# A two-layer attention kernel: opening of the first layer reordered, and one row of softmax sums stored per head in the second

## What is computed

```python
x = x + windowed_attention(group_norm(x))   # 16 heads of width 16, windows of 8x8 tokens, shifted by 4
x = x + masked_attention(group_norm(x))     # 16 heads; 8 look back, 8 look ahead
```

## Time and profile before

| | |
|---|---|
| median of 3 runs | 1255.33 us (1239.32 to 1261.03) |
| the profiled execution, its own time | 1246.15 us |
| its span, first to last instruction | 1244.4 us |
| TensorE busy | 1161.2 us (93%) |
| VectorE busy | 944.2 us (76%) |
| ScalarE busy | 636.4 us (51%) |
| GpSimd busy | 209.5 us (17%) |
| first layer | 0 to about 553 us |
| second layer, first matmul to end | about 562 to 1244 us |
| first to last store of `ots` | 622.4 to 1226.1 us |

### The profile page before, as it was taken

The page is one execution under the profiler, slowest core; times in us unless marked ns, Lnnn a source line. Parts: engine busy times, 40 slices in busy tenths (PEclk is TensorE's granted clock), DMA queues, the critical chain, the costliest instruction groups (busy, mean ns, idle before and its releaser), DMA issues.

```text
span 1244.4 us, 50834 instructions
## 1 busy us (share of the span) xinstructions
PE 1161.2 (93%) x21404; PEld 844.7 (68%) x21404; DVE 944.2 (76%) x1687; ACT 636.4 (51%) x1051; POOL 209.5 (17%) x271
## 2 busy tenths in 40 slices
PE   5689999999999999957899999999999999999983
PEld 2557777777777777745667777777777777777752
DVE  2488888888888888753568787787877878778753
ACT  2255656566665565521455555555555555555530
POOL 0001111111111111120122122221222212222120
PEclk9699999999999999996999999999999999999986
DMA  2000000000000000010033433334333333333433
GB/s 82 13 20 21 21 18 17 17 17 17 17 17 17 18 17 3 5 39 1 2 53 74 81 56 70 59 72 79 56 71 60 72 80 56 71 59 72 80 55 82
DMA packets 304605, 53.91 MB, mean 43 GB/s; under 512 B 270724, under 2 KB 303766, under 8 KB 304534
## 3 DMA queue, kind: packets, MB, share of 16 engines
q1 hardware_dynamic: 303480, 52.75, 20.4%
q10 hardware_dynamic: 1056, 0.13, 0.1%
HBM read 27.56 MB, written 25.17 MB: 42 GB/s over the span
## 4 chain that ended last, share of the span: by engine, by line
PE 42%; DVE 5%; issue 3%; SPq 2%; DMA 2%; ACT 1%; DVEq 0%; ACTq 0%
PE psG L998 13%; PE psA L1040 7%; PE psA L1056 5%; PE psG L1020 5%; PE psE L1089 5%; PE psA L1068 4%; DVE of L1196 3%; DVE sums L1191 2%; SPq L952 2%; PE psG L1007 2%; DMA scratch_heads<-ots 1%; DVE cm L1165 1%; PE psE L1079 1%; ACT probs L1111 0%; DMA sums<-scratch_heads 0%
## 5 line engine op out<-in xcount | busy, mean ns | idle before, releaser
L1165 DVE TENSOR_REDUCE cm<-psG 128x4 f32<-128x1024 f32 (+1 forms) x192 | 235.0, 1224 | 136.2 <-PE psG L1020 136.2
L1111 ACT ACTIVATE probs<-psG 128x1024 f32<-128x1024 f32 x192 | 196.3, 1022 | 130.2 <-PE psG L998 129.7
L998 PE MATMUL psG<-stack 32*128 32x256 f32 (+1 forms) x2048 | 221.7, 344 | 11.1 <-DVE cm L1165 6.6
L1227 POOL TENSOR_SCALAR_AFFINE_SELECT probs<-probs 128x1024 f32<-128x1024 f32 x128 | 139.2, 1099 | 519.6 <-ACT probs L1111 519.6
L1007 PE MATMUL psG<-stack 32*128 32x256 f32 (+1 forms) x2048 | 222.4, 345 | 4.3 <-DVE cm L1165 2.4
L998 PEld LDWEIGHTS psG<-stack 32*128 32x128 f32 x2048 | 151.8, 187 | 69.5 <-DVE cm L1165 27.5
L1007 PEld LDWEIGHTS psG<-stack 32*128 32x128 f32 x2048 | 151.3, 187 | 7.4 <-DVE cm L1165 3.3
L768 POOL TENSOR_TENSOR X<-X,probs 128x96 f32 (+5 forms) x128 | 64.1, 530 | 485.6 <-ACT probs L533 485.6
L447 PE MATMUL psA<-probs,xh 128*128 128x512 f32 x256 | 130.0, 635 | 9.6 <-ACT xh L566 5.3
L1056 PE MATMUL psA<-xh,wqk 128*128 128x256 f32 x512 | 126.4, 392 | 5.6 <-DVE xh L1202 5.6
L1191 DVE RECIPROCAL sums<-sums 128x128 f32<-128x128 f32 x128 | 115.7, 929 | 13.2 <-DMA sums<-scratch_heads 13.2
(11 more groups left out here) (132 smaller groups left out, 1906.0 us busy)
## 6 DMA issues: line engine op xcount, KB each, us to landing
scratch_heads<-ots SPq DMA_DIRECT2D x256, 64.0 KB, 3.6
X<-in_xr SPq DMA_DIRECT2D x32, 256.0 KB, 2.6
raw<-scratch_heads SPq DMA_DIRECT2D x32, 256.0 KB, 2.7
sums<-scratch_heads SPq DMA_DIRECT2D x32, 256.0 KB, 3.0
out<-X SPq DMA_DIRECT2D x32, 256.0 KB, 2.9
probs<-in_wqk SPq DMA_DIRECT2D x1, 512.0 KB, 3.8
wv<-in_wv SPq DMA_DIRECT2D x2, 256.0 KB, 4.2
wqk<-in_wqk SPq DMA_DIRECT2D x1, 512.0 KB, 3.7
```

What stands on the lines that cost most here:

```text
L998: last = nc.tensor.matmul(G[:, at:at + b.size], km[i.k][own_rows(r), o, e, b.keys_of(o) * P:(b.keys_of(o) + 1) * P], qm[i.k][own_rows(r), ...
L1111: nc.scalar.activation(weights[i.k][:, b.weights_at:b.weights_at + 1024], G[:, 0:1024], ACT.Exp).then_inc(exp_done, 1)
L1165: nc.vector.reduce_max(slots, scores, AX_X).then_inc(max_done, 1)
L1227: nc.gpsimd.affine_select(out=diagonal, in_=diagonal, compare_op=ALU.is_ge, fill=0.0, base=0, pattern=[[0, QUADS], [0, 2], [sign, P]], cha ...
```

## The change

Opening of the first layer: SP issues image 0 first, then five small constants, image 1, the mask rows, image 2; the seven other constants are issued from ScalarE's queue. `once` becomes a dictionary from steps to functions. The hidden layer's eight matmuls are cut in two: three (`hide_early`) ahead of step -3, five (`hide_late`) ahead of step -2, each behind a wait for the ReLU that frees its bank; the bias product and the transposes of `aqf` follow the five. The 32 products of the table move ahead of step -1 (`tabulate`), its exponential too (`open_table`), its reciprocal into VectorE's step -1 behind `unit_qk` and ahead of the second `add_bias` and `take_max`, and its layout into ScalarE's step -1 (`bias_across` ahead of the squares, `bias_within` ahead of `copy_c`).

Second layer: the memset gives each head one column of ones in place of 16, so row 16 of a head's 32 rows in `ots` holds the sums and the rest zeros. `regroup` issues four transfers per image, each of 17 partitions. `fetch` issues four: for each half of the heads, the row of sums repeated 16 times by a source stride of zero, and the 16 rows of outputs.

```diff
@@ build_network
-    scratch = nc.dram_tensor("scratch_heads", [2, 2, TOKENS // DIM, DIM, HEADS * DIM], F32).ap()
+    scratch = nc.dram_tensor("scratch_heads", [2, TOKENS // DIM, DIM + 1, HEADS * DIM], F32).ap()
@@ layer0, SP
-            for group, done in ((net, c_net), (others, c_in)):
-                for dst, src in group:
+            def small_inputs():
+                for dst, src, done in ((gavg, given["gavg"], c_avg), (scale, given["scale0"], c_scale), (pt, given["points"], c_hid),
+                                       (w1, given["cpb_w1"], c_hid), (b1, given["cpb_b1"], c_hid)):
                     sp.dma_start(dst if isinstance(dst, bass.AP) else dst[:], src).then_inc(done, 16)
...
-            pipeline(sp, images, [(load, 6)], LAGS)
+            pipeline(sp, images, [(load, 6)], LAGS, once={-5: small_inputs, -4: regions})
@@ layer0, TensorE
-            pe.wait_ge(c_net, 16 * len(net))
...
+            pe.wait_ge(c_avg, 16)
...
+            def hide_early():
+                pe.wait_ge(c_hid, 48)
+                for n in range(EARLY):
+                    hide(n)
+                pe.wait_ge(c_qk, 16)
+
+            def hide_late():
+
+                for n in range(EARLY, 8):
+                    pe.wait_ge(a_hid, n - EARLY + 1)
+                    hide(n)
...
+            def tabulate():
+
+                pe.wait_ge(a_hid, 8)
+                pe.wait_ge(made, MADE)
                 for q in range(HALF):
                     part, at = divmod(q * P, WTOK * WTOK // 2)
-                    last = nc.tensor.matmul(G[:, q * HEADS:(q + 1) * HEADS],
+                    last = nc.tensor.matmul(E[:, q * HEADS:(q + 1) * HEADS],
                                             hidden[part][:, at:at + P], w2[:], start=True, stop=True)
...
-                                  (spread_sums, 0)], LAGS, once=(TABLE_STEP, prepare))
+                                  (spread_sums, 0)], LAGS, once={-3: hide_early, -2: hide_late, -1: tabulate})
@@ layer0, ScalarE
+            for dst, src, done in ((wqk, given["wqk0"], c_qk), (ident, given["ident"], c_ident), (w2, given["cpb_w2"], c_out_w),
+                                   (wv, given["wv0"], c_v), (wo, given["wo0"], c_out_w), (bv, given["bv0"], c_out_w),
+                                   (bo, given["bo0"], c_out_w)):
+                act.dma_start(dst if isinstance(dst, bass.AP) else dst[:], src).then_inc(done, 16)
...
+            def rectify_early():
+                for n in range(EARLY - 1):
+                    rectify(n)
+
+            def rectify_late():
+                for n in range(EARLY - 1, 8):
+                    rectify(n)
+                act.wait_ge(summed, 5)
...
             pipeline(act, images, [(lambda i: exponent(i, 0), 0), (lambda i: exponent(i, 1), 0),
-                                   (copy_v, 1), (copy_z, -1), (normalize, 3), (copy_qk, 2),
-                                   (copy_o, 0), (lambda i: square(i, 0), 3), (lambda i: square(i, 1), 3), (copy_c, 1)], LAGS, once=(TABLE_STEP, finish_table))
+                                   (copy_v, 1), (copy_z, -1), (normalize, 3), (copy_qk, 2), (bias_across, 1),
+                                   (copy_o, 0), (lambda i: square(i, 0), 3), (lambda i: square(i, 1), 3), (bias_within, 1), (copy_c, 1)], LAGS, once={-3: rectify_early, -2: rectify_late, -1: open_table})
@@ layer1
-                nc.gpsimd.memset(va[k][:, :, :, DIM:COL], 1.0).then_inc(z_in, 1)
+                nc.gpsimd.memset(va[k][:, :, :, DIM:DIM + 1], 1.0).then_inc(z_in, 1)
...
-    STORES = 2 * QUADS
+    STORES = QUADS
+    LOADS = 2 * CT
@@ layer1, regroup and fetch
-                wait_alone(sp, loaded[i.k], i.plus(-2).dmas(2))
-                for kind in range(2):
-                    for c in range(QUADS):
-                        first = COL * c + DIM * kind
-                        sp.dma_start(scratch[i.k, kind].rearrange("m e (g c j) -> e c g m j", g=QUADS, c=QUADS)[:, c],
-                                     ots[first:first + DIM, :, :].rearrange("e g (m j) -> e g m j", j=DIM)
-                                     ).then_inc(stored[i.k], 16)
+                wait_alone(sp, loaded[i.k], i.plus(-2).dmas(LOADS))
+                for c in range(QUADS):
+                    sp.dma_start(scratch[i.k].rearrange("m e (g c j) -> e c g m j", g=QUADS, c=QUADS)[:, c],
+                                 ots[COL * c:COL * c + DIM + 1, :, :].rearrange("e g (m j) -> e g m j", j=DIM)
+                                 ).then_inc(stored[i.k], 16)
...
-                for kind, dst in enumerate((raw, sums)):
-                    sp.dma_start(dst[:, :, :], scratch[i.k, kind].rearrange("m e x -> (m e) x")
-                                 .rearrange("(f p) x -> p f x", p=P)).then_inc(loaded[i.k], 16)
+                for f in range(CT):
+                    half = scratch[i.k, f * TILE_HEADS:(f + 1) * TILE_HEADS]
+                    sp.dma_start(sums[:, f, :], half[:, DIM, :].unsqueeze(1).to_broadcast([TILE_HEADS, DIM, TOKENS])
+                                 ).then_inc(loaded[i.k], 16)
+                    sp.dma_start(raw[:, f, :], half[:, 0:DIM, :]).then_inc(loaded[i.k], 16)
```

More of the change, by code:

```diff
@@ new lines, in hide_early @@
+            def hide_early():
[7 more added lines that the diff above has]
+                    hide(n)
+                pe.wait_ge(c_out_w, 64)
+                for o in range(CT):
+                    for c in range(CT):
+                        last = nc.tensor.matmul(A[2][:, o:o + 1], wo[:, c, o * P:(o + 1) * P], bv[:, c:c + 1],
+                                                start=(c == 0), stop=(c == CT - 1))
+                last.then_inc(p_bz, 1)
+                pe.wait_ge(c_ident, 16)
+                pe.wait_ge(made, 1)
+                for t in range(TT):
+                    last = nc.tensor.transpose(E[:, t * P:(t + 1) * P], aqf[:, t * P:(t + 1) * P], ident[:, :])
+                last.then_inc(p_cm, 1)
@@ L326, in prepare, with table_read @@
[L326 to L330, removed]
+                pe.wait_ge(d_bz, 1)
+                pe.wait_ge(c_v, 16)
+            def table_read(i):
+                if first(i):
+                    pe.wait_ge(a_tab, 1)
             def scores(i):
@@ L492, in finish_table, with bias_across @@
+            def bias_across(i):
+                if not first(i):
+                    return
                 act.wait_ge(d_tab, 2)
-                by_parity = table.rearrange("p (q o r e) -> p e r o q", q=HALF, o=CT, r=QUADS)
+                for half in range(2):
+                    rows = slice(half * WTOK, (half + 1) * WTOK)
+                    for r in range(QUADS):
+                        nc.scalar.activation(across[rows, r, :, :], by_parity[rows, 1 - half, r], ACT.Exp,
+                                             scale=16.0).then_inc(a_tab2, 1)
+                act.wait_ge(a_tab2, 2 * QUADS)
+                for half in range(2):
+                    rows, other = slice(half * WTOK, (half + 1) * WTOK), slice((1 - half) * WTOK, (2 - half) * WTOK)
+                    act.dma_start(ebias[other, :, :, half * HALF:(half + 1) * HALF].rearrange("p r o q -> p (r o) q"),
+                                  across[rows, :, :, :].rearrange("p r o q -> p (r o) q")).then_inc(tab_in, 16)
@@ L494, in finish_table, with bias_within @@
+            def bias_within(i):
+                if not first(i):
+                    return
                 for half in range(2):
@@ L498, in finish_table @@
                                              ACT.Exp, scale=16.0).then_inc(a_tab2, 1)
[L499 to L505, removed]
             def square(i, t):
@@ L634, in add_bias @@
                     wait(dve, tab_in, 32)
+                    wait(dve, a_tab2, 4 * QUADS)
                 both = (weights[i.k][:, part * 1024:(part + 1) * 1024]
```

109 lines of the change are left out of this document (55 added, 54 removed).

## The result

The changed kernel takes 2660.68 us (median of 4 runs, 2652.39 to 2671.04) against 1255.32 us: a ratio of 2.125, 95% interval 2.114 to 2.137. The profiled execution has a span of 2650.6 us. Predicted were 2568 us, range 2190 to 3400, slower by over 2% with a chance of 0.86.

What follows compares the result with a forecast made beforehand. TensorE bounds both layers' middles, leaving the opening and drain; one-engine stores would slow the second layer's loop. First stores at 609.2, 31 periods of 61.1 (1894), last stores 47.5, end 14.7 + 0.7, plus 1.8: 2568 us, range 2190 to 3400.

Steps and rivals of the forecast that it cites:

- The cut of 17 rows: Second layer's stores: how many of 16 engines carry a 17-row transfer; one engine was given a chance of 0.85.
- The even split: Second layer's stores: as many engines as divide the rows evenly, at most 16, so one engine for 17 rows.
- The rival with unequal shares: Second layer's stores: 17 rows over 16 engines, one with two rows; about 1231 us, chance 0.12.
- The price of a packet: Second layer's stores: 10.4 ns per packet on one engine, so 47.5 us per image, bounds 39.4 to 73.1.
- The low one, 8.5 ns: Lower bound on one engine's packet time in the second layer's stores, from the busy share of 42.3%.
- The high one, 16.3 ns: Upper bound on one engine's packet time, from 16 engines moving 63 GB/s, half of it idle.
- The rest of the loop: Second layer, from the stores' landing to the next stores: 13.6 us, bounds 9.8 and 17.4, against 9.76 before.
- The opening: First layer's start: first scores at 63.4 us in place of 76.58, 13.2 us saved, bounds 8 to 20.
- The delay by ScalarE's 16 activations: Opening: eight activations and two transfers ahead of the squares, eight more ahead of `copy_c`, about 3.2 us late.
- my term of 6 to 8.6: Opening: the five late hidden matmuls on TensorE take 6 to 8.6 us.
- The fetch: Second layer's four loads, eight engines each: hidden in the middle, bare in the drain at +0.7 us.
- my first rival's case: 17 rows over 16 engines: stores 6.5 to 9.8 us, drain 0 to -3.5 + 0.7, about 1231 us, chance 0.12.

Runs made afterwards that it cites:

- experiment 6: The changed kernel with each 17-row store cut into one transfer of 16 rows and one of 1: median 1231.33 us, ratio 0.982 to the kernel before.
- experiment 3: The changed kernel with 18 rows per store in place of 17: median 1230.88 us, ratio 0.984 to the kernel before, span 1225.7 us.
- experiment 9: The 18-row kernel of experiment 3 run again unchanged: ratio 0.979, span 1242.1 us; three gaps of some 5 us each in the first layer's middle.

## Why the prediction was right

**The cut of 17 rows** was the step that decided, and it was put as a choice between two readings of the completion counts. The even split was right, and it carries nearly all of the slowdown: completions of 1, 9, 1 and 7 for 17, 18, 19 and 21 rows, each as computed before the run. The rival with unequal shares is out.

The Trainium skill's rule (DMA: Bandwidth & Descriptors, "Why a DMA increments its semaphore by 16 and not by 1") speaks of the slowest dimension that is "non-size-1", and the one-row transfers of experiment 6 with their four engines agree; my expectation there forgot that word.

**The price of a packet.** I took 10.4 ns from the one slice with busy engines; it is 11.7 ns, at which 52.8 us in place of 47.5 follow. All bounds held, but my reasons for them did not all hold. The low one, 8.5 ns, read the DMA share as occupancy. In the changed kernel one engine worked and the share is 11.1%, where one of 16 is 6.25%: packets of one engine overlap, and their times add up to more than the engine's. The high one, 16.3 ns, did hold idle time, but 28% of it (1 - 11.7/16.3) and not half: 9 engines sustain 49 GB/s (experiment 3), 7 sustain 38, one 5.4, each 5.4 GB/s per engine or 11.7 ns per packet, while 16 got 63 GB/s, 3.9 each. So the 16 engines of the kernel before were held below their own pace by something they share, 1 ns a packet in all. I take it to be how fast packets of 64 bytes are handed out; no run varied that. The slice of 98 GB/s on which I based 10.4 ns was a burst and no measure of a steady pace; the first slices of 18 rows reach 78 as well, before they settle at 49.

**The rest of the loop**: 11.3 us where I took 13.6. TensorE does come back slow, but only part of the way: in the turn at 719.95 (granted clock 0.53 up to 727.4 us, 1.00 behind it) its first burst and the value projection ran slow (3.42 us where the projection took 1.89 in a full-clock turn), and the matmuls behind it were at full speed again. Stores 5.3 us dearer, the rest 2.3 us cheaper: the two errors have opposite signs, and the loop, 63.7 on average, came close to my 61.1 in part by that luck. ScalarE's wait, which I put near 35 us a turn, was 44.5.

**The sum**, redone with what was measured: 603.5 to the first stores, 31 x 63.7 = 1975, last stores 54.6, the end 17.3: 2650.6. Of the 85 us that I was short, 31 x 2.6 = 81 are the loop.

**The opening**: 17.5 us in this execution, not 13.2, inside its bounds. Image 0 took 4.6 us from issue to landing and image 1 5.8 us, where I had carried over 2.85: both queues were busy, with 2.04 MB moved in the first 10 us. Image 1 landed at 9.2 where I had 6.5, and the first projection came at 15.57, 2 us behind my 13.5. From there each step was shorter than its term: the five late matmuls took 4.55 us, not 6 to 8.6 (TensorE was still fast from the projection before them), the second image's projection 2.56 where I carried over 3.69, the table 10.28, not 11.1. The delay by ScalarE's 16 activations, 3.2 us, was there (TensorE idle 3.52 us ahead of the scores). The mechanism was the one described, each slow or fast stretch behind the first projection guessed on the slow side.

That holds for this execution only. Of the nine profiles with the changed opening, four have their first scores at 59.0 to 59.2 us, five at 62.3 to 62.5. The difference arises between image 1's projection (19.4 us) and image 0's transposes (27.6 us, or 30.9), most of it in the five late matmuls: 4.55 us in the four profiles, 6.4 to 6.7 in the five. The second profile of 18 rows:

```profile
22.45 6.36 PE L312 MATMUL psG<-stack,cpb_w 2*128 2x512 f32 x10
62.42 2.02 PE L365 MATMUL psG<-stack 32*64 32x64 f32 x123 [3.52 <-ACT ct L605]
```

The granted clock was 0.71 from 22.4 to 28.8 us there, and 1.00 from 21.8 to 26.4 us in the changed kernel; in both, TensorE came straight from the projection. What decides between the two, no run shows. In the five my term of 6 to 8.6 held, and the opening saves 76.58 - 62.42 = 14.2 us, near the 13.2 forecast.

**The fetch**: hidden in the middle, as said. Eight engines each, from the changed kernel's DMA view of 719.5 to 731 us: 816 packets = 4 x (128 + 8) + 256 + 16. From its first issue to the end of the span 17.3 us passed against 14.7 before: 2.6 us dearer, not 0.7, since its four issues took 0.6 us each, not 0.4, and the last landing came 6 us after the first issue where it had been 3.5. In the 18-row kernel shorter stores don't quite pay for that: from the last stores to the end 1225.7 - 1198.97 = 26.7 us against 25.6 before. With 16 and 1 rows, which is near my first rival's case, it is 1221.4 - 1196.46 = 24.9: of its drain gain, up to 2.8 us net, 0.7 came.

## What to carry to other kernels

Before changing the shape of a transfer, factor its slowest dimension: 16 or a multiple keeps all engines, 18 costs nothing here, 17 or 19 puts everything on one engine. Fewer bytes and half the transfers can be five times slower, and a row of padding can be the cure. Count the completion packets of one transfer in the DMA view; they say how many engines carried it. And look for the closed loop a transfer sits in: a wait of 1.4 us per turn says that there is no reserve, and every us of a slower transfer is then paid once a turn.

The best version here is the opening as changed with 18 rows per store (experiments 3 and 9), or 16 and 1 (experiment 6): 1.6 to 2.1% faster than before, with intervals that together reach from 1.0 to 3.2%. In the first profile of 18 rows the 18.7 us gained are 622.36 - 605.20 = 17.2 up to the first stores, 2.6 in the loops, and 1.1 given back at the end: it is the opening. (Both of these profiles are without the gaps of experiment 9.)

## What the runs showed of the hardware

- One DMA engine stores packets of 64 bytes from on-chip memory to DRAM at a steady 11.7 ns each, 5.4 GB/s, whether 1, 7 or 9 engines are at work and whether one queue or two feed it. With 16 engines on SP's queue the pace was 1 ns a packet in all.
- Two queues with transfers that fit one engine each share the same engine.
- The share of DMA time in the profile exceeded one engine's (11.1% against 6.25%): packet times overlap.
- The same five matmuls behind the same work took 4.55 us in four executions and 6.4 to 6.7 us in five, with granted clocks of 1.00 and 0.71 in the two traces read.
- With each store on one engine, an issue held SP's queue for 12.7 us (median of 128 issues; it was 0.8, of 256). The shortest took 0.65.
- TensorE's granted clock had a mean of 0.66 over a loop in which TensorE is idle for 42 of 64 us. Within a turn it rises (windows of the changed kernel from 721.5 us on, columns as in the earlier trace rows, and two rows of its chain of work, as start, us, what; TensorE had waited 42 us before):

```profile
721.50:727.40 5.90, 5.88 (x30) 4.04 (x31) 2.67 (x4) 1.90 (x3) 1.10 (x1) 0.53 0.37 128
727.40:731.00 3.60, 3.60 (x88) 2.69 (x92) 2.02 (x3) 1.51 (x2) 0.00 (x0) 1.00 0.02 5
...
722.33 0.41 PE psG L1059 x2
...
724.15 3.21 PE psA L1129 x8
```

The pair of matmuls at 722.33 takes 0.20 us in the kernel before at full clock, so up to 727.4 us TensorE ran at 1.2 GHz, and behind that at 2.4 GHz.
